# An attention loop with fp32 scores on one core: the order of two transposes, the next scores and the value product within a step

## Time and profile before

| | us |
|---|---|
| median of 3 runs | 3946.67 |
| the runs | 3943.34 to 3949.51 |
| the profiled execution, its own time | 3954.3 |
| its span, first to last instruction | 3952.5 |
| TensorE busy | 3611.4 (91%) |
| VectorE busy | 2219.7 (56%) |
| ScalarE busy | 1585.3 (40%) |
| mean granted clock of TensorE | 0.961 |

### The profile page before, as it was taken

The page is one execution under the profiler, slowest core; times in us unless marked ns, Lnnn a source line. Parts: engine busy times, 40 slices in busy tenths (PEclk is TensorE's granted clock), DMA queues, the critical chain, the costliest instruction groups (busy, mean ns, idle before and its releaser), DMA issues.

```text
span 3952.5 us, 47918 instructions
## 1 busy us (share of the span) xinstructions
PE 3611.4 (91%) x19232; PEld 2133.3 (54%) x19232; DVE 2219.7 (56%) x2875; ACT 1585.3 (40%) x2264; POOL 221.5 (6%) x165
## 2 busy tenths in 40 slices
PE   5989799899999999999999999999999899996988
PEld 2654457445664456644565445654457454573454
DVE  2554565466555565465654756537565475654755
ACT  0442443253433444253542635416343163432523
POOL 0000010001000020000200002000020000200200
PEclk9999999999999999899999999999999999998979
DMA  2011001300013000120011200121001300003020
GB/s 69 9 30 59 3 14 29 91 11 26 15 32 87 19 20 14 61 57 30 14 32 50 45 32 13 30 64 33 32 13 30 87 17 25 13 9 91 17 56 32
DMA packets 129422, 139.61 MB, mean 35 GB/s; under 512 B 78994, under 2 KB 98965, under 8 KB 128533
## 3 DMA queue, kind: packets, MB, share of 16 engines
q1 hardware_dynamic: 129204, 136.56, 12.5%
HBM read 99.48 MB, written 37.03 MB: 35 GB/s over the span
## 4 chain that ended last, share of the span: by engine, by line
PE 80%; DVE 7%; DMA 6%; ACT 4%; issue 3%; SPq 1%; POOL 0%; DVEq 0%; ACTq 0%; POOLq 0%
PE banks L472 14%; PE banks L507 12%; PE banks L522 10%; PE banks L491 10%; PE banks L535 7%; PE banks L653 4%; PE banks L552 3%; DMA x_dram<-exps 3%; PE banks L663 3%; PE banks L654 3%; PE banks L655 3%; PE banks L579 2%; PE banks L602 2%; PE banks L642 2%; DMA recips_dram<-recips 1%
## 5 line engine op out<-in xcount | busy, mean ns | idle before, releaser
L1053 DVE TENSOR_REDUCE neg_max<-banks 128x1 f32<-128x1024 f32 x512 | 602.6, 1218 | 415.7 <-PE banks L491 409.1
L828 ACT ACTIVATE exps<-banks,neg_max 128x1024 f32<-128x1024 f32 x512 | 565.0, 1112 | 209.9 <-DVE neg_max L1053 209.8
L838 ACT ACTIVATE exps_turned<-banks 128x1024 f32<-128x1024 f32 x256 | 262.2, 1024 | 927.5 <-PE banks L507 926.8
L507 PE MATMUL banks<-ident,exps 128*128 128x128 f32 x4096 | 570.3, 283 | 38.5 <-ACT exps_turned L838 19.3
L507 PEld LDWEIGHTS banks<-ident,exps 128*128 128x128 f32 x4096 | 449.3, 143 | 231.0 <-issue 231.0
L491 PE MATMUL banks<-qk_halves 64*128 64x512 f32 x3072 | 444.8, 422 | 87.0 <-ACT exps L828 43.1
L522 PE MATMUL banks<-exps_turned,values 128*64 128x256 f32 x4096 | 503.9, 389 | 15.3 <-DVE exps_turned L1062 8.5
L1062 DVE COPY exps_turned<-banks 128x1024 f32<-128x1024 f32 x256 | 313.1, 1223 | 239.5 <-PE banks L507 239.1
L491 PEld LDWEIGHTS banks<-qk_halves 64*128 64x128 f32 x3072 | 291.2, 193 | 282.6 <-issue 241.0
L1218 DVE SCALAR_TENSOR_TENSOR qk_halves<-banks,qk_halves 128x1024 fp32r<-128x1024 f32 x256 | 312.1, 1222 | 142.1 <-ACT qk_halves L867 140.5
L522 PEld LDWEIGHTS banks<-exps_turned,values 128*64 128x64 f32 x4096 | 278.5, 138 | 171.6 <-issue 64.2
(11 more groups left out here) (149 smaller groups left out, 3408.3 us busy)
## 6 DMA issues: line engine op xcount, KB each, us to landing
x_image<-in_x SPq DMA_DIRECT2D x8, 2048.0 KB, 8.8
recips_b<-recips_dram SPq DMA_DIRECT2D x256, 64.0 KB, 3.6
exps_turned<-in_x SPq DMA_DIRECT2D x32, 512.0 KB, 7.7
x_dram<-exps SPq DMA_DIRECT2D x32, 512.0 KB, 2.6
exps_turned<-x_dram SPq DMA_DIRECT2D x32, 512.0 KB, 20.0
out<-exps_turned SPq DMA_DIRECT2D x32, 512.0 KB, 2.7
attended<-mlp_rows SPq DMA_DIRECT2D x96, 112.0 KB
exps_turned<-in_wo SPq DMA_DIRECT2D x8, 1024.0 KB, 5.3
```

The lines of the kernel that those rows point to most:

```text
L507: mm = pe.transpose(TB[:, kt // 4, kt % 4 * P:kt % 4 * P + P], PB[:, 2 * h + n % 2, kt * P:(kt + 1) * P], IDENT[:])
L828: freed(act.activation(PB[:, 2 * h + n % 2], slot(("s", m, i)), ACT.Exp, bias=NM[:, m:m + 1], accum_out=SS[:, m:m + 1]), ("s", m, i))
L1053: dve.tensor_reduce(NM[:, m:m + 1], slot(("s", m, i)), AX.X, ALU.max, negate=True).then_inc(mx, 1)
```

## The change

On TensorE the first turn of a step is issued before the scores of the next step instead of after them, and the value product after the second turn instead of between the two turns. The order of a step was S(n+1), T0(n), V, T1(n), P, small group; it is now T0(n), S(n+1), T1(n), V, P, small group. In the last step (31), which has no scores, the projection `values(0, i + 1)` now stands between T0 and T1 with V behind T1, where V stood ahead of `values`.

On VectorE the copy of the second turn of step n stands between the two row maxima of step n + 1, where it stood behind them, behind the small work and behind `recips` and `outputs`. In step 31, which has no maxima, the copy keeps its old place. ScalarE's, GpSimd's and SyncE's streams stay as they were, and no instruction, DMA or semaphore is added or taken away.

```diff
@@ -726,14 +726,14 @@
             for i in range(B):
                 piece(0, i)
                 for n in range(STEPS):
+                    turn(n, 0, i)
                     if n + 1 < STEPS:
                         scores(n + 1, i)
-                    turn(n, 0, i)
-                    if n >= 2:
-                        value_product(n // 2 - 1, n % 2, i)
                     if i + 1 < B and n == STEPS - 1:
                         values(0, i + 1)
                     turn(n, 1, i)
+                    if n >= 2:
+                        value_product(n // 2 - 1, n % 2, i)
                     if piece_of(n + 1):
                         piece(n + 1, i)
                     if i and n == 1:
@@ -1304,8 +1304,11 @@
             for i in range(B):
                 for n in range(STEPS):
                     if n + 1 < STEPS:
-                        for h in range(2):
-                            row_max(2 * n + 2 + h, i)
+                        row_max(2 * n + 2, i)
+                    if n < STEPS - 1:
+                        copy_turned(n, i)
+                    if n + 1 < STEPS:
+                        row_max(2 * n + 3, i)
                     if i and n == 24:
                         weights_turned(i - 1)
                     if i and n == 25:
@@ -1336,7 +1339,8 @@
                         recips(n // 2, i)
                         if n >= 3:
                             outputs(n // 2 - 1, i)
-                    copy_turned(n, i)
+                    if n == STEPS - 1:
+                        copy_turned(n, i)
                     if piece_of(n + 1) and n % 2 == 0:
                         low_piece(n + 1, i)
                     if i and n == 2:
```

## The result

The changed kernel takes **4113.3 us** (median of 4 runs, 4110.2 to 4119.0) against 3948.1 for the kernel before in the same comparison: a ratio of **1.0416, 95% interval 1.0401 to 1.0430**. That is 165 us more. Forecast were 90 more, 4037, with a range of 4010 to 4070. The direction was right and the size was outside the range.

What follows compares the result with a forecast made beforehand. Ordinary steps were taken as TensorE-bound, steps without a piece as gated by ScalarE behind its copy. Images 2 to 6 cost 13.5 us each (4.0 - 2.6 + 1.0 + 10.3 + 0.8); all +90, 4037 us, range 4010 to 4070.

Steps and rivals of the forecast that it cites:

- term A: Ordinary steps: TensorE's 5.64 us of work hides the 4.98 us chain; change 0, with plus or minus 15 us.
- term B: First scores of a pair, three per image: first turn runs in the wait, 0.88 us gained each, -21 us in all.
- term C: Plain steps without a piece, two per image from 1 on: chain 4.49 to 4.98 us, +1.0 per image.
- term D: Steps 24 to 28, images 1 to 7: small TensorE groups wait for later VectorE work; +10.3 us per image.
- The sum above holds as many slow stretches as now: Whole kernel: the +90 us sum assumes no more TensorE half-clock stretches than before the change.
- The rival on the clock: Images from 1 on: two waits each bring half clock, slowing one scores and one turn; +31 us, 4068; chance 0.12.
- term E: Start of images 1 to 7: later scores and turns, including 1.14 us added behind the log rows; +4.0 us per image.
- term F: End of an image: last copy stands behind outputs that wait for the later V; +0.8 us.

Runs made afterwards that it cites:

- the filler: Changed kernel plus useless TensorE transposes in the waits of steps 24 to 28, images 1 to 7: 4071.5 us, ratio 1.0316 to the kernel before.
- later passes: GpSimd's two pixel passes released two steps later: on the changed kernel 4057.3 us, on the kernel before 3933.8 us.
- the early turns at the borders: Kernel before, first turn ahead of the scores and second right behind them in steps 7, 15, 23: 3949.5 us; with GpSimd's passes released later 3917.5.

## Why the prediction was right in direction and wrong in size

- *Ordinary steps (term A), right.* The chain grew to 4.98 as worked out (exp of head 1 starts 3.62 after sigma, for 3.63) and stayed hidden; the steps cost 0.04 more, 5.4 us in all, inside the bound given.
- *Pair borders (term B), right*: -19.9 for -21.
- *The chain in plain steps without a piece (term C), right at full clock*: scores 25 at 6.53 for 6.57. Scores 31 cost +12 for 3.5: the half clock of the steps before reaches into them (20 us of it, none before); with the filler there is none, and the two together are +6.6 for +7.
- *Steps 24 to 28 (term D), the failed step.* Its queue part was right as far as the runs can tell: +66 with the filler, for +70, or 61 to 73 less the added half clock. What failed is the sentence "The sum above holds as many slow stretches as now". Filling the idle time gained 42 us; in the profiled executions scores 26 to 30 alone fell by 41. The rival on the clock named this with a chance of 0.12 and a price of 31 us; the price was too low. It counted one scores and one turn per stretch, and the prediction took the half clock to come after sample and similarities. It begins inside them: already in the kernel before, sample's row took 8.6 to 11.5 us and that of similarities 8.9 to 10.1 over images 1 to 7, and with waits ahead of them they take 10.9 to 12.9 and 10.2 to 13.1. The evidence taken against it, scores at 1.65 after a wait of 2.38, was one place of seven: in images 3 and 4 the kernel before already had half clock there (scores 10 after 8.8 us).
- *The log rows (term E), the second failed step.* I took "6.28" as what the rows cost and added 1.14 behind it. The copy's new place added that much, but the rows themselves went to 8.12, because all six copies now begin under GpSimd's first pass (the rows start 2.6 us after it, where it was 4.6). Before, two of them were short (0.53 and 0.41; the last one fell between the two passes); now the shortest takes 1.32. Copy and rows together are 2.96 us at scores 9, 21 us in seven images; half clock after the longer wait added the other 9.5 at scores 10. Measured +30.2 for +8. The evidence was in the trace of before: the last image has the same six copies at 1.70 us.
- *Starts of images (term E without the rows)*: +14.6 for +19. *Ends (term F)*: about +2 for +6; no run separates what paid for the rest.
- *Range.* Its top, 4070, allowed for two slow stretches of 2.2 us an image (31 us). Scores 26 to 30 had 37, scores 9 and 10 22 and scores 25 and 31 8 us more than the forecast, some 68 in all.

What stays open is when the clock falls inside the small groups. Fillers and later passes together gave 4031.2 where the sum of the two is 4015 (4113.3 less 98), since scores 26 to 30 had 184 us of half clock in place of 123 with the waits filled in the same way; no run here controls that moment.

## What to carry to other kernels

When a change makes TensorE idle, price the work behind the wait, at half clock, and not only the wait: here waits of 1.4 to 3.6 us cost another 42 us, and useless transposes in them were a gain. Before a row's duration is carried over to another time, look for the same row with other neighbours; the six copies at 1.70 us in the last image would have shown that the 6.28 belonged to GpSimd's overlap, and moving that overlap took 16 us off the kernel before, as much as the early turns at the borders did beside it. A reordering pays where a wait already exists (the pair borders), and costs where small work of another engine is queued behind what was moved.

## What the runs showed of the hardware

Useless work gave clock back: behind a wait of 1.75 us a group of 64 small matmuls took 12.2 us in image 2, and with 16 transposes in that wait 8.6; over images 1 to 7 its row was 10.9 to 12.9 us with the wait and 8.8 to 10.8 with the transposes (9.4 to 11.6 in the run with the later passes too). The Trainium skill, "TensorE: Matmul & The Clock Gate", section "Why this matters for your kernels", warns of idle gaps between bursts of matmuls, though only of longer ones than most of these. The runs agree in kind, with 42 us for filling the four or five waits in each of seven images; and they show half clock in such groups with no wait ahead of them too (17 to 24 us an image from scores 25 to scores 30 of the kernel before). VectorE's bf16 copies of 64x512 within SBUF took 0.28 and 0.41 us alone and 1.3 to 1.5 us while GpSimd multiplied fp32 in SBUF (0.53 where a copy began late in one of its instructions), each ending just after one of GpSimd's instructions; VectorE's reads of PSUM (maxima of 1.20 to 1.23 us) showed no change beside the same passes.
